# Gated cross-attention block on one core: W computed and kept transposed, both normalisations applied on ScalarE, two buffers for the weight sums, two reordered sequences in the last stage

## The reference, cut to what matters

```python
x = x + tanh(g_xattn[0]) * xattn(layernorm(x), ctx, ctx, Wh, wg_w, wo_w, gamma, beta)
x = x + tanh(g_ffn[0]) * ffn(layernorm(x), gate_w, up_w, down_w, gate_s, up_s, down_s)

def xattn(x, k, v, Wh, wg_w, wo_w, gamma, beta):      # 64 sequences of 128 tokens, width 512, 4 heads
    Q, K, V = (per head: x @ Wh[h], k @ Wh[h], v @ Wh[h])
    A = maximum(abs((Q K^T / sqrt(128) * decay).sum(over the 64 sequences)), 1.0)
    O = A @ V                                         # per head
    Y = (O - mean(O)) / sqrt(var(O) + 1e-3) * gamma + beta     # over the 512 columns of a token
    W = relu(x @ wg_w)
    return W * Y @ wo_w

def ffn(x, ...):                                       # hidden width 1408
    return ((silu(x @ gate_w.T * gate_s) * (x @ up_w.T * up_s)) @ down_w.T) * down_s
```

## Time and profile before

| | before |
|---|---|
| median of 3 runs | 1638.23 us (1635.74 to 1641.7) |
| the profiled execution | 1638.45 us, its span 1636.6 us |
| PE / PE weight load busy | 1528.0 us (93%) / 1267.6 us (77%) |
| DVE / POOL / ACT busy | 1203.6 us (74%) / 773.5 us (47%) / 531.5 us (32%) |
| mean granted clock of TensorE | 0.981 |

### The profile page before, as it was taken

One profiled execution on the slowest core, in us unless ns is written; L12 is line 12 of the kernel. 1 busy time (PEld: TensorE's weight loads), 2 busy tenths in 40 slices (PEclk: granted clock), 3 DMA queues, 4 the chain that ended last, 5 costly groups with the idle time before them and its releaser, 6 DMA issues.

```text
span 1636.6 us, 20455 instructions
## 1 busy us (share of the span) xinstructions
PE 1528.0 (93%) x7226; PEld 1267.6 (77%) x7226; DVE 1203.6 (74%) x1686; ACT 531.5 (32%) x807; POOL 773.5 (47%) x796
## 2 busy tenths in 40 slices
PE   6999899899798999999899999999898898898999
PEld 5888788787686878888777778887686786786887
DVE  6677666778687999898796879755568568568672
ACT  4444333343221313232131322223343343343342
POOL 4556556551463646565464645523135135136135
PEclk9999999999999999999999999999999999999999
DMA  7777777665886676767675767663651642642332
GB/s 249 262 268 270 264 238 244 212 223 178 273 237 168 208 210 201 212 216 195 185 214 160 223 192 226 163 174 122 155 181 64 155 161 75 149 176 78 117 116 78
DMA packets 367399, 306.46 MB, mean 187 GB/s; under 512 B 259328, under 2 KB 268928, under 8 KB 367104
## 3 DMA queue, kind: packets, MB, share of 16 engines
q1 hardware_dynamic: 367296, 305.14, 61.1%
HBM read 200.75 MB, written 117.31 MB: 194 GB/s over the span
## 4 chain that ended last, share of the span: by engine, by line
PE 49%; DVE 22%; DMA 8%; issue 7%; SPq 7%; POOL 4%; ACT 2%; DVEq 0%; POOLq 0%; ACTq 0%
PE ps L1586 16%; PE pyb L1483 9%; PE po L1586 6%; SPq L415 5%; PE ps L1518 5%; PE pyb L1586 4%; DVE raw L960 4%; DMA wy_scratch<-misc 3%; PE po L1483 2%; DVE misc L957 2%; PE ptb L1586 2%; DVE op L1021 2%; PE ptb L1483 2%; DMA v_scratch<-tmp 2%; DVE tmp L1110 2%
## 5 line engine op out<-in xcount | busy, mean ns | idle before, releaser
L1335 POOL TENSOR_SCALAR rs<-mv 128x1 f32<-128x1 f32 x192 | 51.1, 266 | 384.2 <-DVE mv L858 138.5
L1586 PE MATMUL ps<-reg,gate 128*128 128x512 f32 x704 | 177.9, 395 | 19.5 <-DVE tmp L1110 10.0
L1586 PE MATMUL ps<-op,wbuf 128*128 128x512 f32 x704 | 179.3, 398 | 16.7 <-DMA wbuf<-ws_scratch 16.7
L1483 PE MATMUL pyb<-xreg,reg 128*128 128x512 f32 x720 | 181.8, 402 | 0.8 <-DVE xreg L882 0.7
L1403 POOL TENSOR_TENSOR reg<-tmp,reg 128x512 fp32r<-128x512 f32 x88 | 125.6, 1428 | 110.4 <-ACT reg L673 110.4
L1387 POOL TENSOR_TENSOR p5b<-p5b,p1b 128x512 f32<-128x512 f32 x44 | 56.9, 1294 | 253.9 <-ACT p5b L697 253.9
L1586 PE MATMUL ps<-reg,up 128*128 128x512 f32 x704 | 173.9, 389 | 0.0
L1586 PE MATMUL ps<-xreg,reg 128*128 128x512 f32 x704 | 165.0, 391 | 7.5 <-POOL reg L1403 4.7
L1586 PEld LDWEIGHTS ps<-op,wbuf 128*128 128x128 f32 x704 | 135.1, 192 | 46.2 <-DMA wbuf<-ws_scratch 18.0
L1586 PEld LDWEIGHTS ps<-reg,gate 128*128 128x128 f32 x704 | 131.1, 190 | 50.5 <-DVE tmp L1110 13.4
L1586 PEld LDWEIGHTS ps<-xreg,reg 128*128 128x128 f32 x704 | 131.0, 188 | 37.6 <-POOL reg L1403 4.7
(11 more groups left out here) (140 smaller groups left out, 2851.7 us busy)
## 6 DMA issues: line engine op xcount, KB each, us to landing
wbuf<-ws_scratch SPq DMA_DIRECT2D x44, 896.0 KB, 4.7
xr<-in_x SPq DMA_DIRECT2D x63, 512.0 KB, 5.1
raw<-in_ctx_t SPq DMA_DIRECT2D x32, 512.0 KB, 4.9
w_scratch<-tmp SPq DMA_DIRECT2D x64, 256.0 KB, 4.2
v_scratch<-tmp SPq DMA_DIRECT2D x64, 256.0 KB, 3.7
raw<-v_scratch SPq DMA_DIRECT2D x32, 512.0 KB, 5.0
raw<-w_scratch SPq DMA_DIRECT2D x64, 256.0 KB, 3.8
x_scratch<-xr SPq DMA_DIRECT2D x32, 512.0 KB, 4.5
```

What stands on the lines that cost most here:

```text
L1335: e.tensor_scalar(dst, var, eps, None, ALU.add).then_inc(s["eps"])
L1483: last = e.matmul(dst, lhs[a], rhs[b], start=(k == 0 and i == 0), stop=(k == n - 1 and i == 2))
L1586: last = e.matmul(dst, l, r, start=(k == 0 and i == 0), stop=(k == n - 1 and i == 1), skip_group_check=sums)
```

## The change

**W transposed.** `w(t)` multiplies a 128-column block of wg (as the stationary operand) with all four tiles of the group's x, so that it gives one block of the transposed W for 512 tokens; the count and size of matmuls are the same. `w_store` and `w_load` follow, the latter with one load for each pair instead of one for each tile.

**Y.** `y_normal` on ACT reads `po` and writes the normalised O to `nbuf`: scale is the power `rs`, bias is `nm`, minus mean times power, which two further POOL instructions make (`minus_mean`). `y_blocks` or `y_t` transpose that, `y_pair_affine` (four ACT instructions of 128x256) or `y_affine` (four of 128x128) apply gamma and beta, which are now one value for each partition, and one DVE instruction multiplies by W. The DVE's `y_scaled` and `y_second` are gone. `norm2` of pairs 2 to 31 is two ACT instructions (`norm2_pair`) with `nm2`. From pair 2 on, the powers are made for two tiles at once (`y_rstd_pair`, `rstd2_pair`).

**Pieces.** There are 12 instead of 13. `y_stats` of both tiles is piece 0, `y_normal` 1, both blocks 2, `y_out` and `y_in` 3, `w_load` 4, affine 5, product and high half 6, low half still 7, `wo_mm`, `x1`, `stats2` and the powers 8 instead of 9, `norm2_pair` 9, blocks 10, `x2_out` 11 instead of 12. The loads `x2_in` of group 0 and the first `x2_pair_hi` and `x2_pair_lo` there stand one step earlier.

**Weight sums.** Two buffers; fill u waits for the store and look of fill u-2.

**Stage D.** The four `pair_in` of a round stand at j = 2, 4, 6, 8 behind `weights_in` instead of all at j = 3 before it; in the downs `finish(t + i)` stands ahead of `prepare_beside(m + 1, i)`.

The diff, cut to its core:

```diff
-    return [(q, n - first_step(q)) for q in range(2, B // 2) if 0 <= n - first_step(q) <= 12]
+    return [(q, n - first_step(q)) for q in range(2, B // 2) if 0 <= n - first_step(q) <= 11]
...
-        sums = over("sums", "wyt0", 0, [128, 6, 4, 128])
-        lowacc = over("lowacc", "wyt0", 12, [128, 768], u32)
+        sums = [over(f"sums{i}", "wyt0", 12 * i, [128, 6, 4, 128]) for i in range(2)]
...
-                e.dma_start(w_s[:, t, :], tmp[:, t % 2, :]).then_inc(s[f"wst{t % 2}"], 16)
+                e.dma_start(w_s[t // 4, :, t % 4, :], tmp[:, t % 2, :]).then_inc(s[f"wst{t % 2}"], 16)
...
+                p.wait_ge("wst0", 32 * (q // 2 + 1))
+                p.wait_ge("wst1", 32 * (q // 2 + 1))
+                e.dma_start(wt_of(q), w_s[q // 2, :, :, 256 * (q % 2):256 * (q % 2) + 256]).then_inc(s[f"wl{q % 2}"], 16)
...
                     for q, piece in pieces(15 * g + step):
-                        if piece == 12:
+                        if piece == 11:
                             x2_out(q)
                             x1_store(q)
                         if piece == 3:
-                            wy_out(2 * q)
-                            if q + 1 < B // 2:
-                                w_load(2 * q + 2)
+                            y_out(q)
+                            y_in(q)
                         if piece == 2 and q + 2 < B // 2:
                             v_load(q + 2)
                         if piece == 4:
-                            wy_out(2 * q + 1)
-                            if q + 1 < B // 2:
-                                w_load(2 * q + 3)
-                            wy_in(q)
-                        if piece == 6:
+                            w_load(q)
+                        if piece == 5:
                             x_again(q)
-                    if g + 1 < NS and step == (9 if g else 11):
+                    if g + 1 < NS and step == (9 if g else 10):
                         x2_in(2 * g + 2)
-                    if g + 1 < NS and step == (12 if g else 14):
+                    if g + 1 < NS and step == (12 if g else 13):
                         x2_in(2 * g + 3)
...
                     n = NI * m + j
-                    if j == 3 and m + 1 < NP:
-                        for i in range(4):
-                            pair_in(q + 4 + i)
...
@@ -581,6 +582,8 @@
                         weights_in(n + 2)
                     if j == NI - 1 and m + 1 < NP:
                         weights_in(n + 3)
+                    if j in (2, 4, 6, 8) and m + 1 < NP:
+                        pair_in(q + 3 + j // 2)
...
 
+            def y_normal(t):
+
+                p.wait_ge("o", t // 2 + 1)
+                p.wait_ge("nm", t + 1 if t < 4 else t // 2 + 3)
+                p.wait_ge("mv", B + t // 2 * 2 + 2)
+                if t >= 6:
+                    p.wait_ge("wyb", t - 5)
+                elif t >= 2:
+                    p.wait_ge("tbw", t - 1)
+                e.activation(nbuf[:, t % 2, :].rearrange("p (a n) -> p a n", a=2), po[:, :, t % 2, :], ACT.Identity,
+                             bias=nm[:, t % 8:t % 8 + 1], scale=rs[:, t % 8:t % 8 + 1]).then_inc(s["nr"])
...
+            def affine(dst, src):
+
+                for k in range(4):
+                    last = e.activation(dst[:, k, :], src[:, k, :], ACT.Identity, bias=colsb[:, 2 * NI + 6 + k:2 * NI + 7 + k],
+                                        scale=colsb[:, 2 * NI + 2 + k:2 * NI + 3 + k])
+                last.then_inc(s["aff"])
...
+            def y_pair_affine(q):
+                p.wait_ge("wyl", 64 * (q - 1))
+                affine(turned[0], turned[0])
...
+            def norm2_pair(q):
+                for t in (2 * q, 2 * q + 1):
+                    p.wait_ge("nm2", q - 1)
+                    if t >= 6:
+                        p.wait_ge("x2b", t - 5)
+                    else:
+                        p.wait_ge("tb2", t - 1)
+                    e.activation(xn[:, t % 2, :], xr[:, t % 4, :], ACT.Identity, bias=nm2[:, t % 8:t % 8 + 1],
+                                 scale=rs2[:, t % 8:t % 8 + 1]).then_inc(s["xn2"])
...
-            def y_second(t):
-                p.wait_ge("y1", t + 1)
-                p.wait_ge("rs", B + t + 1)
-                e.scalar_tensor_tensor(y_to(t), y_to(t), rs[:, t % 8:t % 8 + 1], beta, ALU.mult, ALU.add).then_inc(s["y2"])
-                p.wait_ge("y2", t + 1)
-                p.wait_ge(f"wl{t % 2}", 16 * (t // 2 + 1))
-                e.tensor_tensor(raw[:, 2 + t % 2, :], raw[:, 2 + t % 2, :], y_to(t), ALU.mult).then_inc(s["wy"])
+                e.transpose(tbuf[:, t % 2, :], nbuf[:, t % 2, :]).then_inc(s["wyb"])
+
+            def wy_mul(t):
+                p.wait_ge("aff", t + 1)
+                p.wait_ge(f"wl{t // 2 % 2}", 16)
+                wt = tile_of(wt_of(t // 2), t)
+                e.tensor_tensor(wt, wt, tile_of(turned[0], t), ALU.mult).then_inc(s["wm"])
+
+            def wy_pair_mul(q):
+                p.wait_ge("aff", q + 3)
+                p.wait_ge(f"wl{q % 2}", 16 * (q // 2 + 1))
+                e.tensor_tensor(wt_of(q), wt_of(q), turned[0][:, :, :], ALU.mult).then_inc(s["wm"])
 
...
                     for q, piece in pieces(15 * g + step):
                         t = 2 * q
-                        if piece == 11:
+                        if piece == 10:
+                            x2_blocks(t)
                             x2_blocks(t + 1)
-                        if piece == 10:
-                            norm2(t)
-                            norm2(t + 1)
-                            x2_blocks(t)
-                        if piece in (2, 3):
-                            y_second(t + piece - 2)
-                            wy_blocks(t + piece - 2)
+                        if piece == 6:
+                            wy_pair_mul(q)
+                        if piece == 2:
+                            y_blocks(t)
+                            y_blocks(t + 1)
+                        if piece == 0:
+                            y_stats(t)
+                            y_stats(t + 1)
                     for q, piece in pieces(15 * g + step):
                         t = 2 * q
-                        if piece in (0, 1):
-                            y_stats(t + piece)
-                            y_scaled(t + piece)
-                    for q, piece in pieces(15 * g + step):
-                        t = 2 * q
-                        if piece == 9:
+                        if piece == 8:
                             x1(t)
...
                 for i in range(7):
+                    finish(t + i)
                     if m + 1 < NP:
                         prepare_beside(m + 1, i)
-                    finish(t + i)
...
+            def minus_mean(dst, mean, std, name):
+
+                e.tensor_tensor(dst, mean, std, ALU.mult).then_inc(s["eps"])
+                powers[0] += 1
+                p.wait_ge("eps", powers[0])
+                e.tensor_scalar(dst, dst, -1.0, None, ALU.mult).then_inc(s[name])
...
-                to = [sums[:, 0:(6, 5)[half], o, :] for o in range(4)]
+                to = [sums[u % 2][:, 0:(6, 5)[half], o, :] for o in range(4)]
                 p.wait_ge("wld0", 32 * (k + 1))
                 p.wait_ge("wld1", 32 * (k + 1))
-                p.wait_ge("sst", 16 * u)
-                p.wait_ge("sand", 4 * u)
+                if u >= 2:
+                    p.wait_ge("sst", 16 * (u - 1))
+                    p.wait_ge("sand", 4 * (u - 1))
...
-                    last = three(pw(t), [q[:, k, 128 * (t % 4):128 * (t % 4) + 128] for q in xnt[t // 4 % 2]],
-                                 [q[:, k, :] for q in wgs], k, 4)
+                    last = three(pw(t), [q[:, k, 128 * (t % 4):128 * (t % 4) + 128] for q in wgs],
+                                 [q[:, k, :] for q in xnt[t // 4 % 2]], k, 4)
...
-                            if piece == 9:
+                            if piece == 8:
                                 wo_mm(2 * q, range(4))
                                 wo_mm(2 * q + 1, range(4))
```

211 lines of the change are left out of this document (114 added, 97 removed).

## The result

The changed kernel takes 1611.88 us (median of 4 runs, 1608.08 to 1613.94) where the kernel before takes 1637.53 in the same session: 0.9837 of its time, 95% interval 0.981 to 0.9865. It is faster by 26 us, not by the 55 that were forecast. The profiled execution took 1608.08 us with a span of 1606.3, the fastest of its four, so against the span of 1636.6 before it shows 30.3 us.

The account below looks back on a forecast made before the run. PE was taken as the bound, with DVE second. From 1638.45 us, terms -9.2, +10, -6, -5, -23.2 and -21.8 gave 1583.2 us (chance 0.60, own range 1570 to 1597); the range 1560 to 1608 had 0.81.

Parts of the forecast that it names:

- Stage D: Last stage: spread loads end PE's waits for wbuf, -23.2 us; finish first in the downs, -21.8 us; clock gains included.
- Stage B: Longer chain for four tiles delays PE's low halves, +10 us; bounds +5 and, if the clock falls three times, +16.
- Stage A: Two buffers for the weight sums: PE's waits for POOL go, -5.8 us, and half clock behind two, -3.4; -9.2 together.
- without it PE's three waits close: Stage A: each POOL wait exceeds the PE wait it leads to, so removing it ends PE's three waits, -5.8 us.
- Start of C: Second transposed pair one step earlier: PE's 5.70 us wait shrinks, -5.0, clock -1.5, other waits +0.5; -6 us, bounds -9 to +4.
- Rest of C: Stage C from group 1: less late DVE against new wo_mm waits, -5 us; bounds -16 to +15.
- The term of -13 for late DVE: Rest of stage C: of PE's 15.9 us waiting for hidden, finish and hidden_lo, nearly all late DVE, 13 go.
- +8 = 20 x 0.4: Rest of stage C: wo_mm at piece 8 waits 0.4 us for POOL's low half in 20 of 30 pairs.
- The fourth rival: Stage C: ACT stands behind y_in ahead of the next silu, making PE wait; about 1646 us, chance 0.04.
- The first (POOL as late as before): Stage C: wo_mm waits for POOL's low half come to 44 us instead of 8; 1619 us, chance 0.13.
- The second and third: Second: everything is covered, 1564 us, chance 0.12. Third: stage D's activation loads still delay weights, 1606 us, chance 0.09.
- The fifth, the shared port: Stage C: DVE's paired product stands behind POOL's SBUF pass; at most 5 us, to 1588, inside the forecast's 0.60.

Follow-up runs that it names:

- x2_first: Changed kernel with the x2_in loads ahead of the pair's y_in in their step on SP, for groups 1 and later; 1598.3 us, 0.9784 of before.
- one_sums: Changed kernel with one buffer for the weight sums, as before, all else as changed; 1616.2 us, 0.9875 of before.
- pool_first: Changed kernel with the pair's low half of W*Y ahead of the hidden tile's low half on POOL; 1595.9 us, 0.9758 of before.
- before_d_x2: Kernel before with the new stage D and x2_in first in its step on SP, Y*W as before; 1577.3 us, 0.9645 of before.
- v_on_dve: Changed kernel with the low halves of V's pairs on DVE instead of POOL; 1607.6 us, 0.984 of before.
- best2: Changed kernel, mended orders: W*Y low half first on POOL, x2_in first on SP in every group, sums' low bits a group later; 1578.6 us, 0.9655 of before.
- best4: best2 with the third O product moved forward and copies of weights between scratch memories in group 1 instead of group 0; 1578.2 us, 0.9653 of before.

## Why the prediction was wrong

The mechanism was right in stage D and stage B. What failed stands in the terms for stage A, the start of C and above all the rest of C.

**Stage D (-45; measured -43.1, and 40 by itself)** was right in both mechanisms, and in size in part by luck. The waits fell by 28.6 us, from 35.4 to 6.8, where 33.4 were forecast: one wait of 2.2 us a round is left at the place that was named, where two splits stand together, and not 0.7. PE's busy time, which holds the clock, fell by 14.5 (454.4 to 440.0) where the clock terms had 11.6.

**Stage B (+10; measured +12.3)** was within its bounds. The first output product comes 2.9 us later against the start of the stage (2.5 forecast), the affine takes 1.5 us (1.6). PE's waits there are 9.2 us against 1.8 before, 7.4 more, and the clock, which was in the bounds but not in the value, takes the rest: 13.6 us at about half clock where before had none. In x2_first, the same stage B without half clock, the waits are 11.8 us, 10.0 more than before, which is the value of the forecast.

**Stage A (-9.2; measured -3.4, or 2.1 by one_sums).** The step that failed is "without it PE's three waits close": it compared POOL's wait with PE's and did not ask what DVE would do at that time. DVE had the low bits of the same buffers to look at, which now run against the sums. PE's 5.8 us for POOL went, and 3.4 came back at L934 and 1.5 at L925. The clock term can't be credited to these waits either. The stretches at half clock near 205 and 304 us are gone in the changed kernel, but in one_sums, where the waits for POOL are back, they are gone too.

**Start of C (-6; measured -3.3).** PE's wait for the second pair fell from 5.70 to 3.24 us and not to 0.7. The step that failed: the pair was moved one step earlier on every engine, and on SP its load then stood behind `v_load`, issued at 508.85. The clock behind the wait did not go either: PE is busy 5.95 us at half clock from 518.15 (these count in the rest of C), where before had 3.02. And where +0.5 was left for the rest, PE waits 4.16 us for the low half of the first pair.

**Rest of C (-5; measured +7.2),** half of the miss. At the same cuts, before:

```profile
512.50:1142.80 630.30, 609.14 (x2785) 502.44 (x2785) 525.04 (x731) 164.62 (x223) 333.49 (x338) 1.00 0.68 192
```

PE's idle time is 24.5 us instead of 21.2 and its busy time 613.0 instead of 609.1. The term of -13 for late DVE came in number: of the waits for `hidden`, `finish` and `hidden_lo`, 15.9 us in the earlier trace rows, 2.7 are left. Two steps failed.

The first is "+8 = 20 x 0.4". The mechanism, the low half behind `hidden_lo` on POOL with one step of slack less, is what came, and in 20 places, 17 here and 3 at the start; but the waits are 15.1 us here, 12.9 more than before, and 5.1 at the start. Pair 12 had the low half at 661.81, 2.0 us ahead of the next step; I shortened it and kept its start. In the changed kernel, at pair 6, it starts 1.2 us ahead. pool_first shows that 12 of the 15 us hung on the order of two instructions.

The second is a term put at nothing: what `y_in`, with its own wait, does on SP to the load of x2 behind it. The waits for the low half of V are 6.7 us, 4.7 more than before, with the stall of 5.4 at 800 us among them, and PE is busy 3.9 us longer, with 6.8 us at half clock behind the stall and 6.8 behind the wait at the cut. The fourth rival saw `y_in` ahead of ACT and not ahead of `x2_in`.

Under both lies the reading "nearly all late DVE", which took DVE for full. The earlier trace rows held the other half: 37.6 us of idle before L1005, waiting for ACT, which waited for SP's load. An engine that idles 37.6 us and has PE waiting 12 us for it isn't full; it is blocked. before_d_x2 shows that 16 us of this stretch go when only SP's order changes, more than the 13 of the term.

**The rivals.** The first (POOL as late as before) is nearest to what happened, at 20 us of waits instead of 44. The second and third did not come. The fourth, ACT behind `y_in`, came in one pair of some kernels: in the kernel with mended orders ACT stands 6.0 us for it and PE 4.87 from 482 us. The fifth, the shared port, is real and costs nothing there, by v_on_dve; the place where it did cost was stage A, for which I had not thought of it.

What isn't settled is whether the new Y*W path can be worth anything. With the load first in both, the new one is 10.5 us faster in the rest of C and 13.9 slower in B and 4.1 faster in A (best2 against before_d_x2, one profiled run each); whether the old stage B can stand ahead of the new stage C was not tried, nor another order on POOL in the kernel before.

## What to carry to other kernels

Before crediting a change with relieving an engine, look at that engine's own idle time in the same stretch: if it waits there for another queue, follow the chain to the first engine that stands before you shorten anything, here SP with a load behind an unrelated wait. When a step is moved on engines that run in order, list for each of them what now stands directly ahead of it and when that one's own input comes. And when a buffer is doubled so that two engines can work at once, ask whether they can.

## What the runs showed of the hardware

In two places DVE and POOL, both working in SBUF, took turns rather than shared. DVE's product of 1024 columns took 1.23 us alone and 2.35 from 534.83, when POOL's line 1424 ran from 533.69 to 536.10: it ended 1.08 us after POOL did. POOL's sum from 196.91 took 2.22 us, ending 1.44 us after the DVE instruction that had started before it (196.54 to 197.69), and 1.56 in the kernel with one buffer. The Trainium skill (SBUF — State Buffer, section SBUF: two separate sides) says of the port pair that the two engines share that it is an exclusive lock, and that whichever starts first has it for the whole instruction. The trace agrees to within 0.2 us in both cases.

A store that takes 0.38 us to issue took 3.75 us directly behind two copies between scratch memories, at both places to which these were put (best2 at 468.14, best4 at 548.99), and 4.50 in the changed kernel. It is not the store: in the changed kernel a load of W behind two copies took 2.94 us, from 455.64, where the same load takes 0.75 at 785.20, and SP's next issue came at 458.62.

The clock fell in stage B for 13.6 us in all in one kernel and not at all in another whose stage B is the same code (x2_first). The second had more waits there, 11.8 us against 9.2, and its stage B is still 2.4 us shorter, so a few microseconds of any single profile there are not the kernel's. The stretches of the changed kernel in stage B and after the stall:

```profile
387.60:394.40 6.80, 4.81 (x11) 3.79 (x12) 3.54 (x7) 3.18 (x6) 2.39 (x8) 0.50 0.00 0
...
804.00:810.80 6.80, 5.32 (x19) 4.75 (x20) 4.80 (x9) 1.59 (x2) 4.44 (x4) 0.50 0.62 198
```
